# Diagonal block and second operand of step 32 loaded in the first quarter of step 31, slot copies of steps 32 and 33 placed in front of two evictions

## The reference

```python
h = max(layernorm(x), 0)
x = x + relu(L_norm @ (h @ W0))          # L_norm = I - D^-1/2 relu((adj + adj.T)/2) D^-1/2
h = max(layernorm(x), 0)
out  = diag(adj) @ (h @ W[0]) + triu(adj, 1) @ (h @ W[1]) + tril(adj, -1) @ (h @ W[2])
x = x + out + bias
```

## Time and profile before

| | us |
|---|---|
| median of 3 runs | 961.22 (960.61 to 963.35) |
| the profiled execution | 959.76 |
| its span | 958.0 |
| TensorE busy in the span | 907.2 (95%) |
| VectorE busy | 554.1 (58%) |
| ScalarE busy | 492.7 (51%) |
| GpSimd busy | 288.2 (30%) |

### The profile page before, as it was taken

One profiled execution on the slowest core, in us unless ns is written; L12 is line 12 of the kernel. 1 busy time (PEld: TensorE's weight loads), 2 busy tenths in 40 slices (PEclk: granted clock), 3 DMA queues, 4 the chain that ended last, 5 costly groups with the idle time before them and its releaser, 6 DMA issues.

```text
span 958.0 us, 17229 instructions
## 1 busy us (share of the span) xinstructions
PE 907.2 (95%) x4471; PEld 765.4 (80%) x4471; DVE 554.1 (58%) x1465; ACT 492.7 (51%) x1042; POOL 288.2 (30%) x284
## 2 busy tenths in 40 slices
PE   3657999999999999999999998999999999999998
PEld 2547778888888888888888887888888888888886
DVE  3896777787877775666565655543343343334432
ACT  2898566766666665555545554343333333333331
POOL 4883345344444444444443442111111100000000
PEclk9999999999999999999999999999999999999999
DMA  9995899999999985665556555676665655555552
GB/s 284 328 273 158 273 344 331 315 349 335 344 330 322 331 300 158 187 180 164 165 181 185 167 164 181 198 219 181 188 193 182 187 168 167 164 167 160 159 170 68
DMA packets 181689, 213.73 MB, mean 223 GB/s; under 512 B 13712, under 2 KB 116112, under 8 KB 179600
## 3 DMA queue, kind: packets, MB, share of 16 engines
q1 hardware_dynamic: 138928, 159.23, 55.0%
q10 hardware_dynamic: 42720, 54.01, 16.2%
HBM read 145.04 MB, written 68.16 MB: 223 GB/s over the span
## 4 chain that ended last, share of the span: by engine, by line
PE 85%; DVE 4%; ACT 3%; DMA 2%; issue 2%; SPq 2%; POOL 1%; DVEq 0%; ACTq 0%; POOLq 0%
PE psAcc L535 23%; PE psAcc L533 23%; PE psAcc L534 23%; PE psA L422 3%; PE psG L502 2%; PE psG L504 2%; PE psG L503 2%; PE psZ L464 2%; PE psW L394 1%; DMA colb<-in_adj 1%; DVE sring L833 1%; DMA xp<-in_x 1%; SPq L236 1%; ACT hst L565 1%; PE psAcc L547 1%
## 5 line engine op out<-in xcount | busy, mean ns | idle before, releaser
L599 ACT ACTIVATE Lh<-C 128x512 fp32r<-128x512 f32 x256 | 161.4, 631 | 295.8 <-PE psAcc L535 232.0
L533 PE MATMUL psAcc<-Xh,Lh 128*128 128x512 f32 x512 | 205.7, 402 | 1.8 <-issue 1.4
L533 PE MATMUL psAcc<-Yh,Lh 128*128 128x512 f32 x512 | 200.8, 392 | 0.0
L535 PE MATMUL psAcc<-Xh,Ll 128*128 128x512 f32 x512 | 200.4, 391 | 0.0
L535 PE MATMUL psAcc<-Yh,Ll 128*128 128x512 f32 x512 | 200.1, 391 | 0.0
L534 PE MATMUL psAcc<-Yl,Lh 128*128 128x512 f32 x512 | 199.9, 390 | 0.0
L534 PE MATMUL psAcc<-Xl,Lh 128*128 128x512 f32 x512 | 199.8, 390 | 0.0
L775 DVE TENSOR_TENSOR Ll<-C,Lh 128x512 fp32r<-128x512 f32 x128 | 90.8, 711 | 142.3 <-ACT Lh L599 142.1
L535 PEld LDWEIGHTS psAcc<-Xh,Ll 128*128 128x128 f32 x512 | 96.1, 188 | 21.0
L535 PEld LDWEIGHTS psAcc<-Yh,Ll 128*128 128x128 f32 x512 | 96.1, 188 | 20.4
L533 PEld LDWEIGHTS psAcc<-Xh,Lh 128*128 128x128 f32 x512 | 96.2, 188 | 19.8 <-issue 2.6
(11 more groups left out here) (120 smaller groups left out, 1329.1 us busy)
## 6 DMA issues: line engine op xcount, KB each, us to landing
C<-at_dram SPq DMA_DIRECT2D x128, 256.0 KB, 2.7
at_dram<-AT SPq DMA_DIRECT2D x16, 1088.0 KB, 5.5
R<-in_adj SPq DMA_DIRECT2D x64, 256.0 KB, 6.2
C<-in_adj SPq DMA_DIRECT2D x64, 256.0 KB, 5.3
s_dram<-C ACTq DMA_DIRECT2D x64, 256.0 KB, 5.3
g_dram<-g ACTq DMA_DIRECT2D x32, 512.0 KB, 4.0
C<-s_dram SPq DMA_DIRECT2D x64, 256.0 KB, 3.9
t_dram<-x ACTq DMA_DIRECT2D x32, 256.0 KB, 2.5
```

What stands on the lines that cost most here:

```text
L533: mm(acc, lh, rh[:, kd, :], start=k == 0, stop=False)
L535: mm(acc, ll, rh[:, kd, :], start=False, stop=c < L1 and k == NB - 1).then_inc(used, 1)
L599: A(Lh[:, q, :], C[:, q, :], ACT.Relu if s.c < L1 else ACT.Copy).then_inc(lhi, 1)
```

## The change

Three edits. SyncE issues `lx` and `g2` of step 32 in step 31 at q = 1, behind `load_next(33, 0)` and ahead of `load_next(33, 1)`, and no longer at the end of the body. ScalarE makes the slot copy of steps 32 and 33 ahead of `gev_out` of batches 2 and 3, where it stood behind them. VectorE makes its slot copy ahead of `t_out` of batches 2 and 3, where it stood behind them and behind `split_lo(nxt, 2)`. From step 34 on the order is as before (there are no evictions there).

```diff
--- before.py
+++ after.py
@@ -310,6 +310,9 @@   (SyncE, body, in the loop over q)
                     if q == 1 and c >= L1 + 2:
                         load_t(t)
+                    if q == 1 and c == L1 - 1:
+                        load_lx(nxt)
+                        load_g2(nxt)
@@ -329,9 +332,6 @@   (SyncE, end of body)
                 if L1 <= c < L1 + 2:
                     load_t(t)
-                if c == L1 - 1:
-                    load_lx(nxt)
-                    load_g2(nxt)
@@ -704,10 +704,12 @@   (ScalarE, body)
+                if L1 <= c < L1 + 2:
+                    slot(t)
                 if 2 <= c < L1 + 2:
                     gev_out(t, 2)
                     gev_out(t, 3)
-                if c >= L1:
+                if c >= L1 + 2:
                     slot(t)
```

## The result

| | before | after |
|---|---|---|
| median, us | 962.42 (10 runs, 960.61 to 965.37) | 959.22 (10 runs, 957.21 to 961.37) |
| ratio | | 0.9971, 95% interval 0.9958 to 0.9983 |
| span of the profiled execution, us | 958.0 | 958.1 |

By the ratio the change wins 0.29%, 2.8 us, with an interval of 1.6 to 4.0 us; the two medians lie 3.2 us apart. The forecast was 2.1 us less, 959.1, counted from the 961.22 of the first three runs of the kernel before; over ten runs that kernel has 962.42.

The account below looks back on a forecast made before the run. TensorE, busy 95% of the span, was taken as the bound, so only its gaps count: 1.63 + 1.53 + 0.58 = 3.74, less 1.46 and 0.15, saves 2.13 us, from 961.22 to 959.1; range 957.1 to 961.6.

Parts of the forecast that it names:

- The gaps and their causes: TensorE loses 1.63 us ahead of step 32's psG, 1.53 and 0.58 at starts of steps 33 and 34; late loads, slot copies.
- What is late next: Ahead of psG in step 33: the t_dram chain through result to hTl arrives late, a new gap of 1.46 us.
- the landing's relief: Step 32's t_dram load: lx and g2 of step 33 issued ahead of its crowd shorten its landing by 0.1 us.
- gap 1: Step 32, TensorE ahead of the first psG product: 1.63 us lost waiting for the late lx and g2 loads, claimed gone.
- The first rival: Step 32's t_dram load, uncrowded, lands in about 2.6 to 3.3 us; all gaps go but 0.15; 3.6 us saved; 20%.
- The second rival: VectorE's moved copy in step 32 meets GpSimd or starts late; t_out 1.1 us later; only 0.9 us saved, 960.3; 15%.
- The slower rival: Step 32's t_dram store and load take 10.6 us instead of 7.5; psG of step 33 late; 1.0 us slower, 962.2; 6%.
- Step 34: split_lo of its last quarter, behind a t_dram load, comes too late for TensorE's block: 0.15 us handed back.
- The sum: Over steps 32 to 34: 3.74 us of TensorE gaps less 1.46 and 0.15 handed back, 2.13 us saved.

Follow-up runs that it names:

- loads only: The change without its slot edits: only the two loads moved, ScalarE and VectorE as in the kernel before; ratio to before 0.9971 (0.9955 to 0.9987).
- slots only: The change without its SyncE edit: only the slot copies moved, loads still at the end of step 31; ratio to before 0.9997 (0.9979 to 1.0016).
- g store late: The full change, with step 32's g_dram store issued in step 33 behind split_hi of step 34's first quarter; ratio to before 0.9977 (0.9963 to 0.9990).

## Why the prediction was right, and where it was not

**The gaps and their causes**: right, all three gone. The loads, issued at 568.32 and 568.85, landed 2.9 and 3.3 us later, some 6 us before ScalarE asked at 578.4, and the VectorE copy took 0.43 us with GpSimd idle. Step 33 starts 14.28 us behind step 32, where 14.32 was worked out (589.11 - 574.79).

**What is late next**: right in place, and in size by luck: 1.46 us forecast, 1.42 in one profile and 2.21 in the next. Its two terms were both off. I had the landing's relief at 0.1 us; against step 32's start, `result` came at 19.84 and 20.64 us, where 21.1 was worked out (595.9 - 574.79): a relief of 0.5 to 1.3 us more. And I had 3.39 us from `result` to psG, taken from the trace of before; it was 4.51. Against step 32's start, Yl, which hangs on TensorE and not on the load, moved 3.26 us forward (from 24.83 to 21.57, in both profiles), the second `split_lo` only 3.00 in the first profile, and so Yl came first. The two errors nearly cancel in the first profile, and not in the second. The step that failed is "All of this hangs on psG of step 32, so it moves with gap 1 alone". The issue of the t_dram store did so (1.77 us earlier against step 32's start), but from there to `result` the chain got shorter by 1.23 and 0.43 us, where 0.1 was put, and GpSimd's Yl, which the working does not have, moved with TensorE and made the chain from `result` to psG 1.1 us longer. The Trainium skill ("SBUF — State Buffer", the section on the two separate sides) says that a VectorE operation with two SBUF inputs and a GpSimd operation that reads SBUF lock each other out, and that who starts first keeps the ports. I had used it only for the slot copy. By it the new order of Yl and `split_lo` had a price, and the rows agree where the starts are clearly apart: in the change's two profiles, loads only, slots only and g store late GpSimd starts 0.28 to 0.42 us ahead, and the VectorE operation behind it takes 0.8 to 1.1 us more. In the kernel before (599.62 and 599.64: VectorE 0.68, GpSimd 1.85) the starts are too close to test it.

**The first rival** (load out of its crowd, all gaps gone): it did not come about in this change, but its mechanism is real. The crowd that mattered was not the stores but the two reads issued just ahead on the same queue; with the load ahead of them it lands in 2.6 us, the shortest of the earlier trace rows. The Trainium skill ("DMA: Bandwidth & Descriptors", the section on the anatomy of one DMA) gives the fit behind the prediction's estimate of 2.6 us for transfers that GpSimd issues, while SyncE issues this one; the measured 2.6 us agrees all the same. **The second rival** saw GpSimd's cost in the wrong place: not on the slot copy, but on the `split_lo` one step on, at just its 1.1 us (in the second profile on lxl). **The slower rival**: a chain longer than 7.5 us by 2.1 was not seen; 8.11 was the longest of the profiles. The profile of slots only did lose 2.3 us of distance, by other ways: the collision and the clock. Its times show no loss (0.9997).

**Step 34**: 0.15 us forecast, 0.24 and 0.21 measured, with the stretched `split_lo` (1.62 us) as in the trace of before.

**The sum**: 2.13 us forecast, 2.18 and 1.45 us of distance in two profiles, 2.8 us (1.6 to 4.0) and about 2.6 in the timed runs. Why the timed gain lies above both distances is open; the interval of the change's second series holds both, that of the first (from 1.6) only the 2.18. That the median, 959.22, stands so close to the forecast 959.1 is partly luck: the forecast started from 961.22, which is 1.2 us below the median of ten runs.

**Left open**: why store to result came out at 7.6 to 8.1 us in all five profiles with the slot copies at the old places or the loads at the end of step 31, and at 6.4 to 7.3 in the seven that have both edits and SyncE's old order at the end of step 32. In the five the store landed in 2.0 to 2.5 us and the load took 5.0 to 5.6. In the seven either the store took 2.0 to 2.3 and the load 3.9 to 4.1, or the store 3.9 to 4.1 and the load 3.1. Twelve profiles that divide so cleanly are hardly chance, but no run shows the cause, nor why one kernel's store lands now in 2.1 and now in 3.9 us.

## What to carry to other kernels

When a stall is taken out, look at every queue that was just in time behind it and list what each of its parts hangs on. Here the part that hangs on TensorE moved by 3.26 us, the part behind the transfers by 3.00 and 2.20, and two operations that passed each other before can meet. Where TensorE waits for one operation, it is worth moving that operation ahead of others in its in-order chain: with hTl two places behind `result` nothing was lost ahead of psG in four profiles, with store to result between 6.54 and 8.11 us. The position of a load in its queue counts too: two reads issued just in front cost it 1.3 to 1.5 us.

## What the runs showed of the hardware that was not expected

- The granted clock fell to 0.50 for 3 us after one stall of 2.44 us in a step that otherwise ran without a gap, and cost some 1.6 us more. In the change's second profile a stall of 2.05 us at the same place left it at 1.00.
- A VectorE operation with one operand in PSUM (hTl) kept its 0.68 us beside a GpSimd subtraction; the next, with both in SBUF, was stretched from 0.29 to 1.08 us.
- Issuing a 512 KB store 3.4 us later, behind the load instead of ahead of it, changed the load's chain by nothing that shows (6.48 us against 6.36 and 7.16; the load itself 4.0 us against 3.9 and 3.1).
- Two 256 KB reads issued just ahead on the same queue made a 256 KB load land in 3.9 to 4.1 us instead of 2.6; issued 2.2 to 2.4 us behind the second of them it landed in 3.1.
